# A recommendation tower on one core: the first layer with k outermost and begun while z is made, its bias as a weight row, a ring of three tiles for the embeddings, one-hot products half a chunk ahead, and nine one-hot tables with 17 gathered

## The reference

```
e   = stack([tbl_f[ids[:, f]] for f in range(26)], axis=1)      # B x 26 x 128
sd  = einsum('bfd,bd->bf', e, dense)
ss  = einsum('bfd,bgd->bfg', e, e);  pairs = ss[:, iu, ju]      # 325 pairs, i < j
h   = concat([dense, sd, pairs, dense], axis=1)                 # B x 607
h   = max(h @ W_top1 + b_top1, 0)                               # 607 x 512
h   = max(h @ W_top2 + b_top2, 0)                               # 512 x 256
y   = h @ W_top3                                                # 256 x 1
```

## Time and profile before

| | us |
|---|---|
| median of 3 runs | 405.61 |
| lowest, highest run | 402.92, 405.91 |
| the profiled execution | 404.94 |
| its span, first to last instruction | 403.1 |
| mean granted clock of PE, as a share of full | 0.949 |

### The profile page before, as it was taken

One profiled execution on the slowest core, in us unless ns is written; L12 is line 12 of the kernel. 1 busy time (PEld: TensorE's weight loads), 2 busy tenths in 40 slices (PEclk: granted clock), 3 DMA queues, 4 the chain that ended last, 5 costly groups with the idle time before them and its releaser, 6 DMA issues.

```text
span 403.1 us, 14210 instructions
## 1 busy us (share of the span) xinstructions
PE 337.3 (84%) x6216; PEld 301.7 (75%) x6216; DVE 234.1 (58%) x702; ACT 204.8 (51%) x289; POOL 277.5 (69%) x295
## 2 busy tenths in 40 slices
PE   0556889898989889897989899896998989898585
PEld 0545679797878769795979779683987979796384
DVE  0969968682776438680867457670587538640321
ACT  2372545566466534666465553754346654565132
POOL 6777777777777777777777777777777777773000
PEclk9998989999999989999998999998899999899559
DMA  6998233222323214223323325122141323111000
GB/s 166 246 260 261 77 84 96 79 76 83 98 81 78 76 54 110 68 80 81 96 80 79 81 57 121 55 81 78 55 122 54 99 62 81 55 52 36 3 2 1
DMA packets 19118, 35.33 MB, mean 88 GB/s; under 512 B 7168, under 2 KB 8712, under 8 KB 19056
## 3 DMA queue, kind: packets, MB, share of 16 engines
q0 software_dynamic: 9216, 18.89, 17.8%
q1 hardware_dynamic: 9824, 15.52, 13.9%
q10 hardware_dynamic: 16, 0.01, 0.0%
HBM read 34.39 MB, written 0.01 MB: 85 GB/s over the span
## 4 chain that ended last, share of the span: by engine, by line
PE 55%; POOL 12%; ACT 11%; DMA 9%; issue 8%; DVE 3%; SPq 1%; POOLq 0%
PE et_ps L565 23%; POOL rows L290 12%; PE m_ps L525 10%; PE g_ps L486 8%; ACT et L371 8%; PE m_ps L536 6%; PE et_ps L555 5%; DMA et<-tbl_in 5%; DMA rows<-tbl_in,idx 3%; ACT zt_hi L346 2%; PE m_ps L545 2%; DMA idb<-ids_one_hot 1%; DVE one_hot L406 1%; DVE zt_lo L449 1%; DVE z L442 1%
## 5 line engine op out<-in xcount | busy, mean ns | idle before, releaser
L290 POOL DMA_INDIRECT rows<-tbl_in,idx x288 | 276.7, 961 | 89.3 <-issue 84.8
L406 DVE TENSOR_SCALAR one_hot<-idb,first_row 125x256 fp32r<-125x256 int32 x512 | 159.6, 384 | 81.5 <-PE et_ps L565 78.5
L371 ACT COPY et<-et_ps 128x384 f32<-128x384 f32 (+1 forms) x128 | 123.4, 1031 | 97.8 <-PE et_ps L565 76.7
L565 PE MATMUL et_ps<-one_hot,table_hi 125*128 125x256 f32 x512 | 132.7, 297 | 22.2 <-DVE one_hot L406 18.8
L565 PE MATMUL et_ps<-one_hot,table_lo 125*128 125x256 f32 x512 | 127.1, 286 | 0.0
L565 PEld LDWEIGHTS et_ps<-one_hot,table_hi 125*128 125x128 f32 x512 | 100.1, 195 | 29.2 <-issue 20.4
L565 PEld LDWEIGHTS et_ps<-one_hot,table_lo 125*128 125x128 f32 x512 | 100.0, 195 | 0.0
L555 PE MATMUL et_ps<-ident,rows 128*128 128x128 f32 x288 | 51.1, 291 | 16.6 <-DMA rows<-tbl_in,idx 11.9
L486 PE MATMUL g_ps<-et 128*27 128x26 f32 x4096 | 54.0, 193 | 11.4 <-issue 9.2
L486 PEld LDWEIGHTS g_ps<-et 128*27 128x27 f32 x4096 | 45.3, 106 | 23.0 <-issue 15.9
L555 PEld LDWEIGHTS et_ps<-ident,rows 128*128 128x128 f32 x288 | 32.6, 145 | 22.3 <-issue 13.1
(11 more groups left out here) (46 smaller groups left out, 284.5 us busy)
## 6 DMA issues: line engine op xcount, KB each, us to landing
idb<-ids_one_hot SPq DMA_DIRECT2D x32, 256.0 KB
rows<-tbl_in,idx POOLq DMA_INDIRECT x288
et<-tbl_in SPq DMA_DIRECT2D x7, 448.0 KB
xt<-dense_t SPq DMA_DIRECT2D x8, 128.0 KB, 3.9
z<-w_z SPq DMA_DIRECT2D x2, 256.0 KB, 5.9
et<-w SPq DMA_DIRECT2D x1, 512.0 KB, 6.9
gram<-tbl_in SPq DMA_DIRECT2D x1, 448.0 KB
et<-tbl_in SPq DMA_DIRECT2D x7, 52.0 KB
```

The source lines that it names most:

```text
L290: nc.gpsimd.indirect_dma_start(out=rows[:, r, n, :], out_offset=None, in_=tables[GATHERED[k]], in_offset=bass.IndirectOffsetOnAxis(idx[par ...
L371: nc.scalar.copy(dst, src).then_inc(et_copied, 1)
L406: last = nc.vector.tensor_scalar(one_hot[n % 2][0:KP, k, :], idb[0:KP, n // 2 % ID_RING, n % 2, :], first_row[0:KP, 0:1], float(k), ALU.su ...
L565: last = nc.tensor.matmul(ps[:, n % 2 * CH:n % 2 * CH + CH], part[0:KP, n, k, :], one_hot[n % 2][0:KP, k, :], start=k == 0 and part is tab ...
```

## The change

The list of steps becomes `PLAN`, made from one list of a phase, `PHASE`. `later` says to which chunk a step of phase `p` belongs: O0 to O4 to chunk `p + 1`, G4 to G7 and all of the tower to `p - 1`, the rest to `p`. A phase -1 holds O0 to O4 of chunk 0.

- Table 16 joins the one-hot tables: nine, so four pairs and a single one (O8); 17 are gathered. The transposes of 128 samples go in five steps of 4, 4, 3, 3, 3 tables, ten steps a chunk; the `rows` ring has six slots of up to four tables.
- The one-hot slices lie in a ring of 16 (two tables) and are handed over one by one (`oh_ready`, `oh_used`). At step O(n) DVE builds the next table, so at O8 it builds table 0 of the next chunk. The other DVE work follows the same list.
- `et` is a ring of three tiles of 128 samples. A pair's bank is copied in two copies, one a tile.
- The first layer is four steps, one a row block: X0 (dense features), K0, K1, K2, each with all four output blocks (12 products), summed in both banks of `m_ps`. The bias `b_top1` is one more row of `w1_z`, against a column of ones in `z`. Relu and hi part are one instruction of 512 columns for two output blocks, and DVE makes the lo part straight out of PSUM.
- In the last chunk ACT does the z pieces of A1 and A3.
- All gather ids are loaded in two transfers. SP's order at the start is new; among other things the weights `w2`, `w1_again` and the last block of `w1_z` wait for all nine `table_lo`, and the ids of pairs from 4 on (pair 4 is table 8 of chunk 0) follow them. DVE splits the weights at G3 of phase 0.

```diff
-ONE_HOT = (1, 3, 4, 5, 6, 10, 12, 14)
+ONE_HOT = (1, 3, 4, 5, 6, 10, 12, 14, 16)
...
+PHASE = [(step[0], int(step[1:])) for step in (
+    "T0 G4 G5 O5 T1 G6 G7 X0 O6 T2 A0 A1 O7 T3 A2 A3 O8 Z0 Z1 K0 T4 Z2 K1 "
+    "T5 G0 G1 K2 T6 G2 G3 T7 O0 T8 O1 M0 O2 T9 O3 Y0 O4").split()]
+AHEAD = 5
+G_STEPS = 8
+def later(kind, n):
+    if kind == "O" and n < AHEAD:
+        return 1
+    return -1 if kind in "AZXKMY" or kind == "G" and n >= G_STEPS // 2 else 0
+PLAN = [(kind, p + later(kind, n), n) for p in range(-1, NCH + 1) for kind, n in PHASE
+        if 0 <= p + later(kind, n) < NCH]
+SIZES = (4, 4, 3, 3, 3)
...
+ROW_RING = 6
+STAGES = 4
...
+STARTED = [x for x in PLAN if x[0] == "T" or x[0] == "O" and x[2] % 2 == 0]
+SLOT = {x: i for i, x in enumerate(STARTED)}
+EMPTIED = {(kind, c, n - n % 2 if kind == "O" else n): i for i, (kind, c, n) in enumerate(
+    x for x in PLAN if x[0] == "T" or x[0] == "O" and ends_pair(x[2]))}
...
+            def load_ids(pair):
+                c, i = divmod(pair, PAIRS)
+                before, half = divmod(pair - ID_RING, PAIRS)
+                wait(sp, oh_ready, (before * NO + min(2 * half + 2, NO)) * KT)
+                n = min(2, NO - 2 * i)
+                src = ids_one_hot[c:c + 1, 2 * i:2 * i + n, :]
+                sp.dma_start(idb[:, pair % ID_RING, 0:n, :], src.broadcast_to([128, n, CH]))\
+                    .then_inc(idb_in[pair % ID_RING], 16)
...
+            first = TILES * NG
+            sp.dma_start(idx[:, 0:first], ids_gather[:, 0:first]).then_inc(idx_in[0], 16)
+            load_ids(0)
             for n, f in enumerate(ONE_HOT):
+                if n >= STAGES:
+                    sp.wait_ge(table_lo_done, n - STAGES + 1)
                 src = tables[f].rearrange("(p k) d -> p k d", k=KT)
                 sp.dma_start(table[n][0:SPLIT], src[0:SPLIT]).then_inc(table_in[n], 16)
                 sp.dma_start(table[n][SPLIT:KP], src[SPLIT:KP]).then_inc(table_in[n], 16)
                 if n == 1:
+                    load_ids(1)
+                if n == 2:
+                    load_dense(0)
+                if n >= STAGES and n % 2 == 1:
+                    load_ids(n // 2)
+            sp.dma_start(idx[:, first:], ids_gather[:, first:]).then_inc(idx_in[1], 16)
+            load_dense(1)
             for k in range(KZ):
+                src = w1_z[(k - 1) * 128:k * 128, :] if k else w1_dense[0:D, :]
+                sp.dma_start(w1_raw[k], src).then_inc(w_in, 16)
             sp.dma_start(b2s[:, :], b2).then_inc(w_in, 16)
             sp.dma_start(w3s[:, :], w3).then_inc(w_in, 16)
+            sp.wait_ge(table_lo_done, NO)
             sp.dma_start(w2_raw.rearrange("p (k n) -> p k n", n=H2), w2.rearrange("(k p) n -> p k n", p=128))\
                 .then_inc(w_in, 16)
+            sp.dma_start(w1_again, w1_dense[D:, :]).then_inc(w_in, 16)
+            sp.dma_start(w1_raw[KZ], w1_z[(KZ - 1) * 128:, :]).then_inc(w_in, 16)
+            for pair in range(NO // 2, NCH * PAIRS):
+                load_ids(pair)
+                if pair % PAIRS == 0 and pair // PAIRS >= 2:
+                    load_dense(pair // PAIRS)
...
+            for kind, c, n in PLAN:
+                if kind == "O" and n == 0:
+                    wait(act, g_done, (c - 1) * G_BANKS + G_BANKS // 2)
+                    if c == 1:
                         act.wait_ge(table_lo_done, NO)
+                        act.wait_ge(w_ready, W_READY)
...
+                if kind == "O" and ends_pair(n):
+                    act.wait_ge(oh_used, (c * NO + n + 1) * KT)
+                    held = n % 2 + 1
+                    src = et_ps[SLOT["O", c, n - n % 2] % 2][:, 0:held * CH]\
+                        .rearrange("d (f t b) -> d t f b", f=held, t=TILES)
+                    for t in range(TILES):
+                        last = nc.scalar.copy(et_fields(TILES * c + t, NG + n - n % 2, held), src[:, t])
+                    last.then_inc(et_copied, 1)
...
+                if kind == "K" and n == KZ - 1:
+                    if c == 0:
+                        act.wait_ge(w_in, W_LOADS)
+                    wait(act, h2_sums, c)
+                    for half in range(2):
+                        act.wait_ge(h1_sums, 2 * c + half + 1)
+                        nc.scalar.activation(h1_parts[0][:, 2 * half:2 * half + 2, :],
+                                             m_ps[half][:, :].rearrange("p (m b) -> p m b", m=2), ACT.Relu)\
+                            .then_inc(h1_hi_done, 1)
...
+            def build(unit):
+                c, n = divmod(unit, NO)
+                pair = c * PAIRS + n // 2
+                if n % 2 == 0:
+                    dve.wait_ge(idb_in[pair % ID_RING], (pair // ID_RING + 1) * 16)
+                for k in range(KT):
+                    at = unit * KT + k
+                    wait(dve, oh_used, at - OH_RING + 1)
+                    nc.vector.tensor_scalar(one_hot[0:KP, at % OH_RING, :], idb[0:KP, pair % ID_RING, n % 2, :],
+                                            first_row[0:KP, 0:1], float(k), ALU.subtract, ALU.is_equal)\
+                        .then_inc(oh_ready, 1)
+                if unit + 1 < NO:
+                    table_lo_part(unit + 1)
...
+            table_lo_part(0)
+            build(0)
+            for kind, c, n in PLAN:
+                if kind == "O" and c * NO + n + 1 < NCH * NO:
+                    build(c * NO + n + 1)
+                if kind == "G" and c == 0 and n == G_STEPS // 2 - 1:
+                    split_weights()
+                if kind == "G" and n == G_STEPS // 2:
+                    wait(dve, h1_sums, 2 * c)
+                    dve.wait_ge(xt_in[c % 2], (c // 2 + 1) * 16)
+                    split_parts([t[:, :] for t in x_parts], xt[c % 2][:, :], x_hi_done, c + 1, x_split)
+                if kind == "A" and not by_act(c, n):
+                    bank, use = a_use(c, n)
+                    dve.wait_ge(a_done, c * A_USES + n + 1)
+                    for dst, src in z_pieces(n, a_ps[bank]):
+                        last = nc.vector.tensor_copy(dst, src)
+                    last.then_inc(a_free[bank], 1)
+                if kind == "Z":
+                    bank, use = a_use(c, A_BANKS + n)
+                    dve.wait_ge(zt_hi_done, c * KZ + n + 1)
+                    hi, lo = [t[:, n, :].rearrange("z (g q) -> z q g", q=4) for t in zt_parts]
+                    nc.vector.tensor_tensor(lo, a_ps[bank][:, 0:CH].rearrange("z (q g) -> z q g", q=4),
+                                            hi.bitcast(f32), ALU.subtract).then_inc(a_free[bank], 1)
+                if kind == "K" and n == KZ - 1:
+                    for half in range(2):
+                        dve.wait_ge(h1_hi_done, 2 * c + half + 1)
+                        hi, lo = [t[:, 2 * half:2 * half + 2, :] for t in h1_parts]
+                        nc.vector.scalar_tensor_tensor(lo, m_ps[half][:, :].rearrange("p (m b) -> p m b", m=2), 0.0,
+                                                       hi.bitcast(f32), ALU.max, ALU.subtract).then_inc(h1_split, 1)
...
+            def first_layer(c, k):
+                for m in range(4):
+                    for a, b in ((0, 0), (1, 0), (0, 1)):
+                        rhs = zt_parts[b][:, k - 1, :] if k else x_parts[b][:, :]
+                        last = nc.tensor.matmul(m_ps[m // 2][:, m % 2 * CH:(m % 2 + 1) * CH],
+                                                w1_parts[a][:, k, m * 128:(m + 1) * 128], rhs,
+                                                start=k == m % 2 == 0 and (a, b) == (0, 0),
+                                                stop=k == KZ and m % 2 == 1 and (a, b) == (0, 1))
+                    if k == KZ and m % 2 == 1:
+                        last.then_inc(h1_sums, 1)
+            for kind, c, n in PLAN:
+                if (kind == "T" or kind == "O" and n % 2 == 0) and SLOT[kind, c, n] >= 2:
+                    pe.wait_ge(et_copied, EMPTIED[STARTED[SLOT[kind, c, n] - 2]] + 1)
...
+                if kind == "X":
+                    if c == 0:
+                        pe.wait_ge(w_ready, W_READY)
+                    pe.wait_ge(x_split, c + 1)
+                    wait(pe, h1_split, 2 * c)
+                    wait(pe, y_copied, c)
+                    first_layer(c, 0)
+                if kind == "K":
+                    wait_a(c, A_BANKS + n)
+                    first_layer(c, n + 1)
```

More of the change, by code:

```diff
@@ L97, in z_inputs, with a_use, rows_use @@
     return rows + [-1] * (ZW - len(rows))
+def a_use(c, i):
+    use = c * A_USES + i
+    return use % 2, use // 2 + 1
+def rows_use(c, n):
+    i = c * TR_SLOTS + n
+    landed = sum(16 * SIZES[j % TR_HALF] for j in range(i % ROW_RING, i + 1, ROW_RING))
+    return i % ROW_RING, landed
 def wait(eng, sem, value):
@@ L179, in dlrm_tower @@
         a_done = sem("a_done")
-        a_free = sem("a_free")
+        a_free = [sem(f"a_free{i}") for i in range(2)]
         zt_hi_done = sem("zt_hi_done")
@@ new lines, in _ @@
```

(28 more changed lines are left out.)

496 lines of the change are left out of this document (179 added, 317 removed).

## The result

The changed kernel takes 426.58 us (median of 4 runs, 420.95 to 430.55) beside 404.26 for the kernel before on the same chip (402.60 to 405.91): a ratio of 1.047, interval 1.033 to 1.061. A repeat gave 424.48 (421.77 to 429.05, 6 runs), ratio 1.051, 1.045 to 1.057. It is slower by some 5%, 5 to 7 us more than the 419.2 forecast and inside the range of 398 to 429. The profiled execution is the longest of the four, 430.55 us for a span of 428.8, so the shape is read from it and the terms are weighed in the repeat's profile, 422.61 us for 420.8.

The account below looks back on a forecast made before the run. Before, gathers set the pace (45.03 us a chunk), TensorE 2 us behind; after, TensorE's 41.5 of work plus 5.25 of waits. 71.3 + 6 x 46.75 + 65.6 = 417.4 us of span, plus 1.8: 419.2 us, range 398 to 429.

Parts of the forecast that it names:

- T1: T1 directly behind O5 needs the bank of pair O4, O5, copied in two copies of 256 columns: +1.25 us a chunk.
- A0 to K0: VectorE's chain to zt_lo, 9.6 us with handovers, against 6.1 of TensorE's work: 3.5 us lost, some 1.25 at T3, 2.3 at K0.
- O4: O4 needs the copies of pair O2, O3, with only Y0 (0.95 us) between: a wait of +0.35 us.
- O0's 0.15: O0 needs T6's copy, which stands behind the two relu activations on ScalarE: a wait of +0.15 us.
- TensorE's work: Per chunk 39.85 us, +2.1 for the ninth one-hot table, -0.45 for fewer transposes: 41.5 us.
- The clock: New waits on TensorE may lower its granted clock: taken as 0, bounds 0 and 1.9 us a chunk.
- rival B: Waits and more: gram stops and a low clock add 1.9 us a chunk, 430.6 us; chance 0.17.
- The gram runs: Four runs of 128 gram products a chunk on TensorE: stops taken as 0, bounds 0 and 4 x 1.07 us.
- Start: VectorE leads, with table 8's ids at 47.7 us; O4 of chunk 1 ends and T0 starts at 71.3 us.
- End: From T0 of chunk 7: T9 34.8 us later, then 30.8 behind T9 with 3.0 gained, 65.6 us in all.
- The gathers: On GpSimd, 34 gathers a chunk take 43.0 us instead of 45.6; one 4.5 us stop, last gather starting at 351.
- Rival A: Gathers still set the pace, new waits mostly absorbed: 43.0 us a chunk, 396.7 us; chance 0.17.

## Why the prediction was right, and what it lacked

The mechanism and sign held; the forecast was 5 to 7 us short of the medians. Two terms had been put at nothing, the clock (0.77 a chunk, 4.6 us in the repeat) and the stops (2.3), and an end that came out 3.2 us shorter hid a part of them. Against the repeat's span:

| | forecast | measured |
|---|---|---|
| T0 of chunk 1 starts | 71.3 | 71.1 |
| TensorE's work a chunk, at full clock | 41.5 | 41.5 |
| waits a chunk at T1, A0 to K0, O4, O0 | 5.25 | 4.67 |
| other idle time of TensorE, a chunk | 0 | 0.57 |
| lower clock, a chunk | 0 | 0.77 |
| stops that nothing released, a chunk | 0 | 0.39 |
| period | 46.75 | 47.90 |
| T0 of chunk 7 to the end | 65.6 | 62.35 |
| span | 417.4 | 420.8 |

The period is (358.45 - 71.08) / 6. TensorE is busy 42.27 us of it on average over the six windows, 0.77 above the 41.5 of the two chunks at full clock; the other 5.63 are idle. The stops of 0.97 and 1.36 in the chain are (2.33 / 6) 0.39 of that, and the waits that its timeline shows, 1.26 at T1, 1.26 at T3, 1.84 at K0 and 0.31 at O4, are 4.67. What is left, 0.57, is idle time in pieces mostly too short for a row of their own; the sum had left it out, although the old kernel's 3.0 us had such a rest too. That waits and rest together come to the forecast's 5.25 is luck. The period of 47.9 lies just above the 46 to 47.5 that the prediction gave as its sign of being right.

**T1** "+1.25 us": 1.26 in every chunk. The reason given, two copies of 256 columns after a pair, shows as two copies of 0.71 each (the mean of the 64 copies of 256 columns by form; 1.18 for the two in the chain), and the edit that puts G6 and G7 between takes the wait away. Right.

**A0 to K0** "3.5 us", some 1.25 of it at T3 and 2.3 at K0: 1.26 and 1.7 to 1.9 (2.35 in the first chunk), 3.1 on average. VectorE's chain, priced at 9.5 us, took 8.85 (275.18 to 284.03 in the repeat), as the one-hots took 2.2 and not 2.5. That both waits are one is shown by the run that moved T3 alone. The one-hots of the next table account for 0.5 us of it, by the run that moved them; the 1.24 left at K0 are the rest of the same chain (the pieces of A, then zt_hi and zt_lo), which no run took apart.

**O4** +0.35 measured 0.31. O0's 0.15 is too small to be picked out of the short idle pieces.

**TensorE's work** "41.5": 41.54 and 41.49. The 2.1 for the ninth table and the 0.45 taken off for the transposes held in sum; neither was measured alone.

**The clock**, the step that failed: "three of the four new waits are nearer to those short spells, so I take 0 for the forecast". Each was judged alone against an idle spell in the old trace. The runs show that no length of one wait decides it: with T1's wait gone, or K0's, or only the 0.5 to 0.7 us of it that go with the one-hots of the next table, the clock mostly stays at 1.00. Whether the waits add up, or whether taking one away only shifts the moment at which the others fall, the runs do not tell apart. In four of the repeat's six chunks K0 ran at 1.2 GHz and took 2.93 us instead of 1.70; in the profiled run all six lost something, four of them the same. The 1.9 a chunk of rival B (clock and stops) was near the truth of the profiled run: from 70.2 to 363.6 us the clock took 1.76 a chunk (busy 43.26 on average) and stops 0.41, 2.2 together, with the same 4.7 us of waits, and the execution's 430.55 us is that rival's 430.6, which is luck to that digit: clock and stops were 0.3 a chunk above it, the start 1.1 us below. The medians, 424.5 and 426.6, lie between forecast and rival, so their chances of 0.55 and 0.17 were too far apart. The earlier trace rows held the warning: a wait of 2.27 us with a slow table behind it, where 2.3 was expected at K0. The working counted the four waits and did not weigh the one with TensorE's next products directly behind it.

**The gram runs**: put at 0, bound 1.07 each. Over the whole span TensorE's gram steps waited for nothing visible 5.4 us in the profiled run and 4.3 in the repeat, less than the old kernel's 9.2, so the pairs of steps did not add to them. Most of the four runs a chunk go through. Stops of 0.5 to 1.9 us come in two chunks of six, and there directly behind T7, ahead of O0, and within X0; in gram steps they come at the start, behind T0 of chunk 7 and in the last run. The Trainium skill (Runtime: NRT & Kernel Launch, Instruction fetch mechanics) calls the cost of a new block of instructions mostly hidden; the stops are in keeping with the "mostly", but no run shows that this is their cause.

**Start**: T0 within 0.2 us, in part by luck. The ids were there at 46.3 in the repeat (45.6 in the profiled run), not 47.7, and O4 of chunk 1, which has no M0 and Y0 ahead of it there, waited 1.26 us for the copy of its pair (PE, 69.08), which was not in the sum. **End**: 3.2 us shorter than forecast. T9 of the repeat starts at 392.7, 34.3 us behind T0 (34.8 forecast), so what is off is the tail behind it, 28.1 instead of 30.8. Against the old kernel's 33.8 it gained 5.7 and not 3.0: 2.4 up to the first Z (granted clock 1.00 instead of 0.67, the gram stop 1.94 instead of 2.73), 1.6 from there to the second layer (0.81 instead of 0.64; K0 ran slow, 2.64 us, K1 and K2 mostly fast) and 1.8 behind that, where the prediction had nothing.

**The gathers** set no pace: the last one starts at 380 to 385 us, not 351, because GpSimd waits for TensorE some 25 times and not once. Rival A (396.7 us) did not come, for the reason given, "the order of instructions leaves T1 no cover". Times like its own came with the cover, and with the other edits of those kernels: 396.19 and 394.28. The weight loads' share, by which the Trainium skill (Perfetto Trace Analysis, Identifying the Most-Contended Engine) would have given TensorE room, is 75% before and after; it is work that it counts, and by work there was room, as the faster versions show.

## What to carry to other kernels

When an order of steps is rewritten, price it by who must have finished before each instruction, not by busy shares: two banks in turn, with a step directly behind the one that fills a pair, cost 1.26 us of TensorE's time each time, and independent work put between made it nothing (two gram steps) or 0.4 us (the five transposes of A2 and A3). On the engine that feeds the critical one (here VectorE), work for the next chunk goes behind the work that someone waits for now (0.5 us a chunk, and the clock on top). And a wait of 1.7 us or so on TensorE has a price beyond its length: the products behind it may run at the lower clock. Here removing the one at T1 gave back 1.3 times its length by the medians and twice in the best chunk.

## What the runs showed of the hardware

- The length of one idle spell did not decide the clock. With 1.26, 1.26 and 1.7 to 2.35 us of waiting at T1, T3 and K0 the products behind K0 mostly ran at 1.2 GHz (2.93 us instead of 1.70), yet in the repeat a wait of 1.69 or 1.70 at K0 was followed twice by the full and twice by the lower level. Of the eight such waits in the two profiles of the changed kernel six had slow products behind them; without T1's wait (the runs that moved T1) it was one of seven, at 1.69 to 1.75 us. With T1's wait gone, 2.18 us at K0 left K0 at 1.70 us, and the next step, K1, then took 2.55. Why the same wait ends both ways is open. The Trainium skill (TensorE: Matmul & The Clock Gate, A second HAM failure mode: psum-queue depth-cycling) tells of a clock that oscillates through small idle spells between groups of products in turning PSUM banks, and these runs agree in that it fell to 0.50 with no idle spell above 2.35 us.
- Stops of TensorE that nothing released, mostly 0.5 to 1.9 us long (2.29 at the start of one kernel, 2.22 inside a chunk of the last), appear at the same steps again and again (in the gram step behind T0 of chunk 7: 1.11 us in the profiled run, 1.05 in the repeat, 0.76 with T1 and T3 covered; ahead of O0 in the period of chunk 2: 0.50, 0.97 and 0.71), and in the last gram run in all that show it (1.93 to 2.36 in the changed kernels, 2.73 in the old one).
- Of the indirect gathers, 0.94 us as a rule, some took 2.7 us (GpSimd's line of the changed kernel, columns as in the earlier trace rows):

```profile
L297 POOL DMA_INDIRECT rows<-tbl_in,idx x272: 938/944/2745, 3.3 to 385.5; - x136
```

  Before, the longest took 1.56. The mean is now 1.009 us where it was 0.961; no run shows why. The last gather starts at 385.5 instead of 366.6, since GpSimd waits for free slots.
